# Behind the last scatter: the fifth chunk's sums made and added ahead of the first chunks' output products

## The reference, cut to what matters

```python
Wij = ssp(f_ij @ Wf1 + bf1) @ Wf2 + bf2
x_ij = h[idx_j] * (Wij * rcut_ij[:, None])
agg = segment_sum(x_ij, idx_i, num_segments=n_atoms)
out = ssp(agg @ Wo1 + bo1) @ Wo2 + bo2          # ssp(v) = softplus(v) - log(2)
x = layernorm(x + out)
...
e = leaky_relu(h_att[src] @ a1 + h_att[dst] @ a2, 0.2)
alpha = softmax of e over the edges of each dst
h_neigh = segment_sum((x @ W1_w + W1_b)[src] * alpha, dst)
x = layernorm(x + leaky_relu(x + h_neigh + (x * h_neigh) @ W2_w + W2_b, 0.2))
```

## Time and profile before

| | |
|---|---|
| median of three runs | 1394.67 us (1394.07 to 1395.38) |
| profiled execution, span | 1393.9 us |
| its own time | not listed apart; the median lies 0.8 us above the span |
| PE busy | 1169.1 us (84%) |
| DVE busy | 1197.9 us (86%) |
| ACT busy | 856.8 us (61%) |
| POOL busy | 824.9 us (59%) |

### The profile page before, as it was taken

How to read it: one execution, slowest core, us unless ns; L and a number is a source line. 1 busy time by engine, 2 the same in 40 slices (tenths; PEclk the granted TensorE clock), 3 DMA queues, 4 the chain that set the end, 5 groups by cost and what they waited for, 6 DMA issues and landing times. The chain is left out here.

```text
span 1393.9 us, 27946 instructions
## 1 busy us (share of the span) xinstructions
PE 1169.1 (84%) x9072; PEld 944.0 (68%) x9072; DVE 1197.9 (86%) x2225; ACT 856.8 (61%) x2126; POOL 824.9 (59%) x910
## 2 busy tenths in 40 slices
PE   5786877789999869899889999999999485877895
PEld 4453455457778647787668787777777485877895
DVE  7788976549999869899889999999998279999986
ACT  2564664577788878788888888888875044000023
POOL 3377777777777777777777777777777230000011
PEclk9787998799999999999999999999999798789998
DMA  8232342266897577899698899888887773776661
GB/s 258 81 88 82 89 123 81 80 160 169 241 281 228 171 238 235 224 250 267 178 247 238 247 280 231 255 237 242 254 253 199 189 244 107 237 226 223 226 225 37
DMA packets 246565, 276.09 MB, mean 198 GB/s; under 512 B 35079, under 2 KB 194470, under 8 KB 243078
## 3 DMA queue, kind: packets, MB, share of 16 engines
q1 hardware_dynamic: 200018, 184.96, 44.9%
q0 software_dynamic: 25792, 53.29, 11.9%
q10 hardware_dynamic: 20596, 35.89, 11.3%
HBM read 162.85 MB, written 111.20 MB: 197 GB/s over the span
## 5 line engine op out<-in xcount | busy, mean ns | idle before, releaser
L1970 POOL DMA_INDIRECT edge_rows<-x_rows,pos x806 | 781.4, 969 | 251.8 <-issue 231.5
L1468 ACT ACTIVATE h_edge<-ps_wh,w_col 128x128 f32<-128x128 f32 x808 | 230.0, 367 | 106.4 <-PE ps_wh L1269 98.8
L1313 PEld LDWEIGHTS ps_d<-back_one,back 128*128 128x128 f32 x1914 | 232.7, 193 | 60.7 <-issue 57.7
L1313 PE MATMUL ps_d<-back_one,back 128*128 128x128 f32 x1914 | 241.7, 279 | 4.9 <-DVE agg_t L1787 4.3
L1276 PE MATMUL ps_wh<-wf,filt 128*128 128x128 f32 x1616 | 236.9, 292 | 0.3 <-DVE filt L1570 0.2
L1262 PE MATMUL ps_v<-f_t,wf 128*128 128x512 f32 x400 | 223.5, 642 | 0.0
L1574 DVE TENSOR_TENSOR x_rows<-ps_wh,h_edge 128x512 f32<-128x512 f32 x202 | 138.1, 684 | 91.2 <-DMA edge_rows<-x_rows,pos 48.9
L1276 PEld LDWEIGHTS ps_wh<-wf,filt 128*128 128x128 f32 x1616 | 207.2, 201 | 2.5 <-DVE filt L1570 2.4
L1106 PE MATMUL ps_wh<-yard 128*128 128x150 bf16 x1575 | 138.1, 233 | 60.2 <-DVE yard L1096 36.7
L2436 PE MATMUL ps_wh<-loan,yard 128*126 128x129 f32 x1250 | 156.2, 289 | 37.8 <-DVE yard L2686 29.7
L1106 PEld LDWEIGHTS ps_wh<-yard 128*128 128x128 bf16 x1575 | 109.4, 100 | 105.3 <-DVE yard L1096 77.4
(11 more groups left out here) (342 smaller groups left out, 1435.0 us busy)
## 6 DMA issues: line engine op xcount, KB each, us to landing
c_tab<-yard SPq DMA_DIRECT2D x25, 1575.0 KB
yard<-c_tab SPq DMA_DIRECT2D x25, 1575.0 KB, 6.6
dst_bc<-dst ACTq DMA_DIRECT2D x99, 252.0 KB
back<-edge_rows SPq DMA_DIRECT2D x42, 516.0 KB, 6.6
edge_rows<-x_rows,pos POOLq DMA_INDIRECT x806
back<-edge_rows SPq DMA_DIRECT2D x48, 258.0 KB, 4.5
m_tab<-yard SPq DMA_DIRECT2D x25, 393.8 KB
mask_room<-m_tab SPq DMA_DIRECT2D x5, 1968.8 KB, 12.6
```

Source lines behind the costliest of these rows:

```text
L1313: mm = nc.tensor.matmul(acc(c), back_rows(n)[:, k0 + t, 0:D], back_one[:, m % 2, o + t, :], start=t == 0, stop=t == k1 - k0 - 1, skip_grou ...
L1468: copy = nc.scalar.activation(h_edge[:, j, q, :], ps_wh[:, bank, 1, q * D:(q + 1) * D], ACT.Copy, scale=w_col[:, t(q)])
L1970: return pool.indirect_dma_start(table[s], bass.IndirectOffsetOnAxis(places_here, 0), rows, None)
```

## The change

On PE, `sums(4)` is moved ahead of `z(0)`, and `o1(2)` and `o1(3)` each move up past one `z`. On DVE, `into(4)` is moved ahead of `rows(0)`. No instruction is added or removed, and ACT, POOL and SP keep their order.

```diff
                 sums(2)
                 o1(1)
                 sums(3)
+                o1(2)
+                sums(4)
                 z(0)
-                o1(2)
+                o1(3)
                 z(1)
-                sums(4)
-                o1(3)
                 z(2)
                 turn(0)
                 o1(4)
...
                 into(2)
                 ones(4)
                 into(3)
+                into(4)
                 rows(0)
                 rows(1)
                 normal_rows(0)
-                into(4)
                 normal_rows(1)
                 rows(2)
                 rows(3)
```

## The result

The changed kernel takes 1400.85 us (median of nine runs, 1398.36 to 1403.88) against 1395.74 us (nine runs, 1394.07 to 1397.28) of the kernel before: ratio 1.0037, 95% interval 1.0026 to 1.0048, so 3.6 to 6.7 us slower. The prediction was 1400.4 us.

What follows compares the result with a forecast made beforehand. PE was taken to bound the changed stretch, DVE the masked maxima from 1164.30. Uncovered `softplus(2)` and the chain behind gave +5.7 us: 1394.67 to 1400.4 us, range 1398.6 to 1402.7.

Steps and rivals of the forecast that it cites:

- The ceiling: PE from `sums(3)` on, 39.7 us: idle only 0.00 + 1.02 us, so even a perfect order wins about 1 us.
- The uncovered `softplus(2)`: ACT's `softplus(2)` waits for the later `z(0)`, and `o1(3)` for its Relu: PE stands for 2.6 us.
- the path: Work from the step behind `sums(3)` to the first masked maximum, 38.87 us before; forecast 5.7 us longer.
- The chain behind: Late `rows(1)` delays `z(2)` by 1.2 us, then `softplus(3)`, `o1(4)`, `rows(2)` and `z(3)`.
- the first gap away: Rival, no gap at `o1(3)`: 3.1 us remain, 1397.8 us; chance 0.12, shared with more than 1.0 us given back.
- The sum: Both ends of the path, `s2(0)` and `rows(4)`, 5.6 to 5.7 us late: +5.7 us taken, median 1400.4 us.
- The loads: Mask loads behind `sums(4)` start about 4.5 us earlier, already hidden; rival that they win up to 4.5 us: chance 0.02.
- The clock: Rival: PE's clock falls to 1.2 GHz in the gap at `o1(3)`, adding 1.5 us, 1401.9 us; chance 0.33.

Runs made afterwards that it cites:

- change_again: The changed kernel once more with no edit, on the same chip as other experiments: path 44.63 us, median 1400.27 us, ratio 1.0040 to before.
- into_4_put_back: Against the changed kernel, DVE's `into(4)` again behind `normal_rows(0)`, PE's order kept: path 44.62 us, median 1400.26 us, ratio 1.0034 to before.
- o1_3_back_and_chain_cut: Changed kernel with `o1(3)` behind `z(1)`, ACT's `softplus(3)` ahead of `inverse_deviation(1)`, DVE's `rows(2)` ahead of `normal_rows(1)`: 1396.30 us, ratio 1.0006 to before.

## Why the prediction was right, point by point

- **The ceiling.** PE's rows of before left about 1 us to be won, and no run in which `sums(4)` stood early was faster than before beyond its interval. But that "even a perfect order" could win no more was wrong: the 39.7 us counted there begin at `sums(3)` and leave out the 3.39 us in which PE stood in front of it. The order with `z(0)` in that wait is 4.7 us faster than before.
- **The uncovered `softplus(2)`.** Forecast 2.6 us in front of `o1(3)`, counted between starts of rows; counted so, it is 1132.49 − 1127.68 − 2.20 = 2.61, ended by the Relu as said. (The 2.45 in the bracket count from the end of `z(0)`'s last product, a row of 0.38 us where the next would start after 0.22, so 0.16 less.) Swapping `o1(3)` and `z(1)`, or a third buffer, took 2.5 us from the path: two different edits that both take this wait away.
- **The chain behind.** Forecast 1.2 us in front of `z(2)`; counted between starts, 1137.00 − 1133.63 − 2.20 = 1.17 (1.01 in the bracket). `o1(4)` was forecast 4.27 us after `z(2)` and came after 4.26 (1137.00 to 1141.26), `z(3)` 1.42 after that and came after 1.52. With the first gap away the prediction left 3.1 us and the expectations 3.3; it was 3.25 and 3.24.
- **The sum.** +5.7 forecast, +5.75 and +5.76 measured on the path in two profiles. Its steps are right one by one to within 0.2 us, and small errors cancelled in part: `rows(3)` came 0.25 us later than forecast (`sums(4)`, for one, took 4.54 us instead of 4.46), and `rows(4)` followed it after 3.62 us instead of 3.79. That 1400.4 lies so near the median of 1400.85 is in part luck: the forecast started from a median of three runs, 1394.67, which the nine runs put at 1395.74, 1.1 us higher, while the medians rose by 5.1 us, 0.6 less than forecast (interval 3.6 to 6.7).
- **The loads.** DVE waits for no mask, and its stage is as long as before: hidden already.
- **The clock.** I gave a fall in the gap a chance of 0.33. Three profiles hold this gap of 2.45 us (the change, change_again, into_4_put_back), and in none did the clock fall; filling it with work changed neither path nor median. Three cases don't settle whether the chance was too high, and for the executions without a profile this stays open. The price was bounded too low: the prediction took at most 1.64 us, and in front of `sums(3)` a fall made the same products 1.4 to 2.9 us longer (last section).
- **Hidden in my comparison.** The sum went against one profiled execution in which `sums(3)` ran partly at 1.2 GHz. That it took 3.42 us in one profile and 6.31 in another means that single spans are weak evidence for a difference of 5.7 us; the medians, and the path between two fixed instructions, are better.

## What to carry to other kernels

In an order written by hand, look at what each step's consumer stands behind: moving a long step ahead of a short one is free on its own engine, but the short one's result may start work on another engine that the long step used to cover. Count the cover before and after the move. And where an engine waits, look for a step that needs none of what it waits for: `z(0)` in the wait ahead of `sums(3)` was worth 0.3%, more than any order of the busy stretch behind it that was run.

## What was not expected of the hardware

The granted clock in front of `sums(3)` didn't follow the length of the pause there. It stayed at 1.00 after 3.04 us of standing in the profile of the change and after 3.44 us in o1_3_back_and_chain_cut, and it fell after 2.94 us in into_4_put_back, where `sums(3)` then took 6.31 us. The busy time over that stretch, columns as in rows 2:

```profile
1117.65:1123.40 5.75, 5.75 (x27) 5.75 (x28) 3.40 (x2) 0.00 (x0) 0.52 (x1) 0.50 0.59 229
```

TensorE has work all the time and is granted half its clock, 1.2 GHz. The same 15 products took 3.42 us at 2.4 GHz, so the pause cost 2.9 us more than its length here and nothing in the other two. In eight profiles `sums(3)` follows a pause of 2.48 to 3.77 us: after 3.04 and 3.44 us it took 3.42 us, after 2.48, 2.72, 2.94, 3.10, 3.39 and 3.77 us it took 4.79 to 6.31. The fall stands in the kernel before (3.39 us, 4.79) as in the changed order, and may be a part of the scatter of their runs; no run separates it. In the four profiles with `z(0)` in the pause, where PE stood for at most 1.20 us, `sums(3)` took 3.35 to 3.42 us.
